# Leaf networks of a depth-4 tree layer: all leaves with a mask, or tokens sorted by leaf

## The reference

```python
x = x + L0_attn(layernorm(x))      # 16 heads, causal
x = x + L0_ffn(layernorm(x))       # trees, then attention 128 wide
x = x + L1_attn(layernorm(x))      # 16 heads
x = x + L1_ffn(layernorm(x))

# L0_ffn: three trees q, k, v on x of 4096 tokens x 128
def _fff(x, node_w, node_b, w1, b1, w2, b2):      # depth 4: 15 nodes, 16 leaves
    cur = 0
    for _ in range(4):
        score = x . node_w[cur] + node_b[cur]
        cur = 2 * cur + 1 + (score >= 0)
    sel = one_hot(cur - 15, 16)
    hidden = relu(x @ w1[l] + b1[l]) * sel[:, l]  # w1[l] 128 x 64, all 16 leaves l
    return sum_l hidden[l] @ w2[l] + sel @ b2     # w2[l] 64 x 128
out = softmax(q k^T / sqrt(128)) v                # per batch of 1024 tokens
```

## Time and profile before

| | |
|---|---|
| median of 3 runs | 1783.16 us (1781.45 to 1785.85) |
| the profiled execution | 1783.86 us, span 1782.1 us |
| busy of the span | PE 91%, DVE 85%, ACT 72%, POOL 46% |
| mean granted TensorE clock | 0.943 |
| bytes moved | 141.89 MB |

### The profile page before, as it was taken

The page is one execution under the profiler, slowest core; times in us unless marked ns, Lnnn a source line. Parts: engine busy times, 40 slices in busy tenths (PEclk is TensorE's granted clock), DMA queues, the critical chain, the costliest instruction groups (busy, mean ns, idle before and its releaser), DMA issues. The chain is left out here.

```text
span 1782.1 us, 47495 instructions
## 1 busy us (share of the span) xinstructions
PE 1613.3 (91%) x18834; PEld 1038.2 (58%) x18858; DVE 1518.7 (85%) x2248; ACT 1276.2 (72%) x2523; POOL 817.8 (46%) x1533
## 2 busy tenths in 40 slices
PE   5599999999976999999899549999999999999966
PEld 3376667666665887877688314444444444444544
DVE  8699999999856999988677768999999999999735
ACT  6488878888834444454565628888989898998955
POOL 5488888888845001000340323444444444444446
PEclk9699999999965999999999868999999999999978
DMA  7522222323172766565000351111121121112031
GB/s 247 207 85 86 87 90 87 98 86 98 52 148 45 97 95 91 93 90 69 0 1 1 144 184 47 56 56 55 59 65 59 52 73 51 60 53 71 26 76 48
DMA packets 119910, 141.89 MB, mean 80 GB/s; under 512 B 22221, under 2 KB 80778, under 8 KB 119690
## 3 DMA queue, kind: packets, MB, share of 16 engines
q1 hardware_dynamic: 119258, 138.79, 30.8%
q10 hardware_dynamic: 432, 0.07, 0.0%
HBM read 92.70 MB, written 44.98 MB: 77 GB/s over the span
## 5 line engine op out<-in xcount | busy, mean ns | idle before, releaser
L888 DVE TENSOR_REDUCE heads_mx<-heads_psM 128x1 f32<-128x1024 f32 x512 | 602.1, 1219 | 48.4 <-PE heads_psM L979 32.2
L959 ACT ACTIVATE heads_probs<-heads_psS 128x512 f32<-128x512 f32 x1024 | 546.1, 601 | 77.7 <-PE heads_psS L1002 71.7
L928 POOL TENSOR_TENSOR heads_masked<-heads_probs,g_tri 128x128 f32<-128x128 f32 x512 | 233.7, 456 | 360.8 <-ACT heads_probs L959 360.7
L654 POOL TENSOR_TENSOR heads_probs<-heads_probs,one_ebias 128x256 f32<-128x256 f32 (+1 forms) x512 | 341.6, 689 | 76.8 <-ACT heads_probs L686 76.1
L615 DVE TENSOR_REDUCE heads_mx<-heads_psM 128x1 f32<-128x1024 f32 (+7 forms) x512 | 348.8, 748 | 23.7 <-PE heads_psM L697 23.0
L686 ACT ACTIVATE heads_probs<-heads_psS 128x512 f32<-128x512 f32 x576 | 316.3, 603 | 67.6 <-PE heads_psS L697 62.4
L979 PE MATMUL heads_psM<-three_kS,three_qS 48*128 48x512 bf16 x1024 | 230.4, 395 | 20.5 <-PEq L2050 11.6
L1002 PE MATMUL heads_psS<-three_qS,three_kS 50*128 50x512 bf16 x1024 | 238.0, 389 | 0.7 <-ACT heads_probs L959 0.3
L1510 ACT ACTIVATE trees_hid_hi<-trees_hid 128x512 fp32r<-128x512 f32 x192 | 121.6, 633 | 152.4 <-DVE trees_hid L1531 151.5
L1531 DVE SCALAR_TENSOR_TENSOR trees_hid<-trees_psH,g_b,trees_chosen 128x512 f32<-128x512 f32 x192 | 143.8, 749 | 31.8 <-DMA trees_chosen<-leaf_choice 15.1
L1027 PE MATMUL heads_psO<-heads_probs,heads_ones_only 128*32 128x128 f32 x1920 | 162.0, 284 | 0.0
(11 more groups left out here) (273 smaller groups left out, 3174.3 us busy)
## 6 DMA issues: line engine op xcount, KB each, us to landing
trees_chosen<-leaf_choice SPq DMA_DIRECT2D x96, 256.0 KB, 7.6
head_outputs<-g_small SPq DMA_DIRECT2D x128, 128.0 KB
one_qS<-q_parts SPq DMA_DIRECT2D x128, 96.0 KB
one_kS<-k_parts SPq DMA_DIRECT2D x128, 96.0 KB
three_qS<-q_parts SPq DMA_DIRECT2D x128, 96.0 KB
three_kS<-k_parts SPq DMA_DIRECT2D x128, 96.0 KB
q_parts<-g_w SPq DMA_DIRECT2D x8, 768.0 KB, 4.6
k_parts<-g_w SPq DMA_DIRECT2D x8, 768.0 KB, 5.8
```

The source lines that it names most:

```text
L654: pool.tensor_tensor(pr[:, a:a + w], pr[:, a:a + w], bass.AP(eb.tensor, eb.offset + NEAR - 1, [list(eb.ap[0]), [-1, w]]), ALU.mult).then_i ...
L888: dve.tensor_reduce(mx[:, n % 2, k:k + 1], psM[k % 2][:, :], AXX, ALU.max, negate=True).then_inc(max_taken, 1)
L928: pool.tensor_tensor(masked[n % 2][:, kb, :], probs[n % 2][:, kb, kb * P:(kb + 1) * P], g["tri"][:, 0:P], ALU.mult).then_inc(near_done, 1)
L959: act.activation(probs[n % 2][:, kb, h * CH:(h + 1) * CH], ring.bank(i)[:, :], ACT.Exp).then_inc(slot_taken, 1)
```

## The change

The leaf networks no longer run over all leaves. `add_projected` keeps the normalized tokens `xn` of all chunks and `sel` of all tiles (`one_of`) for the next stage, no longer makes `x_hi`, `x_lo` and the split weights and biases, and no longer stores `leaf_choice`. SP fills three arrays `sorted_inputs` of 6144 x 128 with zeros instead, in nine transfers of 1 MB, and loads the weights behind them; it waits for both before the stage ends.

`sorted_trees` takes the place of `trees`. Products with triangular tables count how many tokens chose each leaf and rank each token within its leaf. The region of a leaf is padded to whole tiles of 128, and `pos` is each token's row in its tree's sorted array. POOL scatters `xn` to those rows by 96 indexed transfers (3 trees x 32 tiles of 128 rows of 512 bytes). SP loads groups of four sorted tiles; the arrays have 6144 rows whatever the counts are, so there are 12 groups per tree, 36 in all. In a group PE turns the four tiles, multiplies each with the one leaf's `w1` (and with `b1n` for the bias), turns the hidden values and multiplies them with that leaf's `w2s`, which has the second bias as row 65; all in full fp32. The column of the leaf's weights comes from a register that PE loads from `leaf_at` (`which`), once for each product with a leaf's weights. DVE copies the outputs, SP stores them to `sorted_outputs`, and POOL fetches them back in token order by 96 indexed transfers. q and k are turned by PE afterwards and go to `qkT`; v goes to `v_tok` directly.

```diff
 def add_projected(nc, m, g, hand, gather, ins):
...
             gather.load_inverse(sp, B - 1)
-            load_weights(1)
-            load_weights(2)
+            sp.wait_ge(cleared, 2)
+            for f, i in itertools.product(range(FF), range(ZERO_PARTS)):
+                sp.dma_start(bass.AP(g["xs_dram"][f].tensor, i * ZEROS, [[ZERO_PARTS * ZEROS, P], [1, ZEROS]]), zeros[:, :]).then_inc(zeroed, 16)
+            for f in range(FF):
+                load_weights(f)
...
-            for c in range(NCH):
-                store_sel(c)
+            sp.wait_ge(zeroed, 16 * ZERO_PARTS * FF)
+            sp.wait_ge(w_loaded, 16 * (4 * FF + 2))
...
                 act.activation(xnT[:, c % 2, :], psT[c % 2][:, :], ACT.Copy).then_inc(xnT_ready, 1)
-                act.activation(g["x_hi"][:, c * CH:(c + 1) * CH], psT[c % 2][:, :], ACT.Copy).then_inc(high_ready, 1)
...
-def trees(nc, m, g):
+def sorted_trees(nc, m, g):
...
+        @block.sync
+            def load(k):
+                if k % GROUPS == 0:
+                    sp.wait_ge(scattered[k // GROUPS], 16 * NT)
+                if k >= NX:
+                    sp.wait_ge(s["x_turned"], k - NX + 1)
+                sp.dma_start(xg[:, k % NX, :, :], rows(g["xs_dram"], k)).then_inc(x_loaded[k % NX], 16)
+            def store(k):
+                sp.wait_ge(s["y_ready"], k + 1)
+                sp.dma_start(rows(g["ys_dram"], k), yg[:, k % NX, :, :]).then_inc(y_stored[k % NX], 16)
+            for k in range(4):
+                load(k)
+            for k in range(ALL):
+                if k + 4 < ALL:
+                    load(k + 4)
+                store(k)
...
+        @block.gpsimd
...
+            pool.wait_ge(s["pos_ready"], 1)
+            for f in range(FF):
+                for t in range(NT):
+                    pool.indirect_dma_start(g["xs_dram"][f][:, :], bass.IndirectOffsetOnAxis(ap=pos[:, f, t:t + 1], axis=0),
+                                            xn[:, t // TPC, t % TPC, :], None).then_inc(scattered[f], 16)
+            for f in range(FF):
+                for u in range(NX):
+                    pool.wait_ge(y_stored[u], 16 * len([k for k in range((f + 1) * GROUPS) if k % NX == u]))
+                for c in range(NCH):
+                    i = f * NCH + c
+                    if f < 2 and i >= NG4:
+                        pool.wait_ge(s["q_turned"], i - NG4 + 1)
+                    for t in range(c * TPC, (c + 1) * TPC):
+                        out, done = (back[:, i % NG4, t % TPC, :], fetched[i % NG4]) if f < 2 else (g["v_tok"][:, t, :], v_fetched)
+                        pool.indirect_dma_start(out, None, g["ys_dram"][f][:, :], bass.IndirectOffsetOnAxis(ap=pos[:, f, t:t + 1], axis=0)).then_inc(done, 16)
...
+        @block.tensor
...
+            def which(j):
+                return pe.value_load(leaf_at[0:1, j:j + 1], min_val=0, max_val=(LEAVES - 1) * LW)
...
+            def first_layer(k):
...
+                for t in range(TPC):
+                    j = k * TPC + t
+                    out = psH[k % 2][:, t * LW:(t + 1) * LW]
+                    pe.matmul(out, of(j), g["b1n"][:, :], start=True, stop=False)
+                    last = pe.matmul(out, xT[:, k % 2, t * P:(t + 1) * P], g["w1"][:, f, bass.ds(which(j), LW)], start=False, stop=True)
...
+            for k in range(ALL + 3):
+                if k < ALL:
+                    turn(k)
+                if 1 <= k <= ALL:
+                    first_layer(k - 1)
+                if 2 <= k <= ALL + 1:
+                    turn_hidden(k - 2)
+                if k >= 3:
+                    second_layer(k - 3)
+            for i in range(2 * NCH):
+                turn_back(i)
```

More of the change, by code:

```diff
@@ new lines, in keep, with fill @@
+            def keep(t, op, fill, base, pattern, down):
+                pool.wait_ge(s["made"], made[0])
+                pool.affine_select(out=t, in_=t, compare_op=op, fill=fill, base=base, pattern=pattern, channel_multiplier=down).then_inc(s["made"], 1)
+                made[0] += 1
+            def fill(t, value):
+                pool.memset(t, value).then_inc(s["made"], 1)
+                made[0] += 1
+            fill(upper[:, :], 1.0)
+            fill(block_upper[:, :], 1.0)
+            fill(member[:, :], 1.0)
@@ L1434, in _ @@
+            pool.wait_ge(v_fetched, 16 * NT)
         @block.tensor
         def _(pe):
[L1436 to L1449 removed]
@@ new lines, in turn_hidden, with second_layer @@
+            def turn_hidden(k):
+                pe.wait_ge(s["hid_ready"], k + 1)
+                if k >= 2:
+                    pe.wait_ge(s["hidT_ready"], k - 1)
+                for t in range(TPC):
+                    last = pe.transpose(psG[k % 2][0:LW, t * P:(t + 1) * P], hid[:, k % 2, t, :], g["identf"][:, :])
+                last.then_inc(s["hid_turned"], 1)
+            def second_layer(k):
+                f = k // GROUPS
+                pe.wait_ge(s["hidT_ready"], k + 1)
+                if k >= 2:
+                    pe.wait_ge(s["y_ready"], k - 1)
+                for t in range(TPC):
+                    j = k * TPC + t
+                    last = pe.matmul(psO[k % 2][:, t * P:(t + 1) * P], hidT[:, k % 2, t * P:(t + 1) * P], g["w2s"][:, f, bass.ds(which(j) * 2, D)],
+                                     start=True, stop=True)
+                last.then_inc(s["out_done"], 1)
@@ new lines, in turn_back @@
+            def turn_back(i):
+                pe.wait_ge(fetched[i % NG4], 16 * TPC * (i // NG4 + 1))
+                if i >= 2:
+                    pe.wait_ge(s["q_taken"], i - 1)
+                for t in range(TPC):
+                    last = pe.transpose(psQ[i % 2][:, t * P:(t + 1) * P], back[:, i % NG4, t, :], g["identf"][:, :])
+                last.then_inc(s["q_turned"], 1)
+            pe.wait_ge(s["made"], MADE)
+            pe.wait_ge(s["made_v"], 2)
+            for t in range(NT):
+                last = pe.matmul(bank[4][0:W, 0:NT + 1], one_of[:, t, :], after[:, NT - t:2 * NT + 1 - t], start=t == 0, stop=t == NT - 1)
@@ new lines, in _ @@
+            last.then_inc(s["counted"], 1)
+            for i in range(4):
+                pe.matmul(bank[i][:, :], upper[:, :], one_of[:, i * 8:(i + 1) * 8, :].rearrange("p t w -> p (t w)"), start=True, stop=True).then_inc(s["ranked"], 1)
+            pe.wait_ge(s["padded_ready"], 1)
+            pe.matmul(bank[5][0:W, 0:1], block_upper[:, :], padded[:, :], start=True, stop=True).then_inc(s["based"], 1)
+            pe.wait_ge(s["reach_ready"], 2)
+            for t in range(NT):
+                for i in range(2):
+                    last = pe.matmul(bank[6][:, t * TREES:(t + 1) * TREES], selT[0:W, t * P:(t + 1) * P], reach[:, i, t, :], start=i == 0, stop=i == 1)
@@ L1549, in attend_wide @@
+            for k in range(ALL + 1):
+                if k < ALL:
+                    take_hidden(k)
+                if k >= 1:
+                    keep(k - 1)
 def attend_wide(nc, m, g):
```

378 lines of the change are left out of this document (176 added, 202 removed).

## The result

| | before | after |
|---|---|---|
| median of 4 runs each, us | 1783.22 (1781.45 to 1785.85) | 2029.29 (2024.58 to 2030.66) |
| ratio, 95% interval | | 1.1374 (1.1351 to 1.1397) |
| profiled execution: span, us | 1782.1 | 2027.3 |
| mean granted clock of the core | 0.943 | 0.823 |
| trees, from their first instruction to the first of the wide attention, us | 291.6 | 539.8 |

The account below looks back on a forecast made before the run. PE was taken to bound the old trees, DVE close behind. The new stage, 35.4 + 112t + 36G = 457.8 us, is 166.2 longer than 291.6; 1783.9 + 166.2 + 7 = 1957 us, range 1850 to 2110.

Parts of the forecast that it names:

- G: Time of one group of four tiles, 36 in all: 8.0 us, from eight register reads at 0.75 plus 2.0 for turns.
- Opening: Start of the new trees stage, counting and ranking until positions exist and scattering can begin: 20 us, given 15 to 26.
- t: POOL's time for one indexed transfer: 1.2 us, with 112 exposed (32 scatters, 80 fetches), 134 us.
- one by one: Rival: POOL takes each indexed transfer to its landing, t = 3.1 us, kernel 2170 us; chance 0.09.
- as quick as SP: Rival: POOL's 112 exposed transfers at t = 0.34 us, with G = 5.4, kernel 1767 us; chance 0.07.
- First load: After the first tree's scatters: the scatter's landing, 2 us, and a 256 KB load, 3.9 us; 6 us together.
- Its clock decides nothing here: In the groups, PE's real work of 5.1 us at 1.2 GHz was said to fit into the 8 us group.
- The cheap reads: Rival: register reads cost 0.2 to 0.5 us, so loads pace the groups at G = 6.4, kernel 1899 us; chance 0.25.
- filling: Three more iterations of the group loop fill and drain the pipeline with part of the work: 4 us.
- The end: Behind the last fetch, before the next stage: the last landing (3.1 us for 64 KB) and the barrier, 4.4 us.
- Routing: Stage before the trees: nine stores of zeros ahead of the weights on SP's queue lengthen it by 0 to +13, taken +7 us.

Follow-up runs that it names:

- e1: The change with the leaf's number a constant, so PE reads no register in the groups and every tile uses leaf 0; 1955.31 us.
- e8: e5 with PE's group work cut: leaf's first weights stationary, hidden layer comes out turned, bias products and hidden turns dropped; 1812.49 us.
- e4: The change with six unread 128x512 bf16 products added to each group on PE, and one bank for the turned hidden layer; 1933.90 us.
- e6: The change with fifty small unread bf16 products added on PE ahead of the groups; 1961.54 us.
- e13: The change with 12 small unread products on PE ahead of the groups, on the third chip; 2032.25 us.
- e14: The change with 50 small unread products on PE behind the last group, on the third chip; 2034.12 us.
- e11: e12 with the scatters issued in one row, without waits for the groups, and q's turns three groups later; 1836.76 us.
- e12: The kernel of e10 unchanged, timed again on the third chip; 1801.21 us, ratio 1.0103 to the kernel before.
- e5: The change with POOL's scatters of trees k and v paced, four for each group PE has turned; 1967.37 us.
- e10: e8 with q and k turned between the groups and v's 32 fetches moved into the next stage, on the second chip; 1738.02 us.

## Why the prediction was right, and where not

The direction, the chain of links and the range held; the number was 3.6% low, 72 us. That the rest of the sum came out to 3 us is in part luck: G was near by a wrong reason, and errors of both signs cancel. By its own steps:

- **Opening**, 20 us said, 13.5 measured. The 64 products before the positions took 1.9 us and not 6.
- **t**, 1.2 said, 1.26 for a scatter and 1.25 for a fetch. The row of POOL's own pass over a tile came out close, SP's 0.34 and the 3.1 of a landing did not; that a transfer (0.96 busy and 0.30 of "issue") costs what a pass costs is a coincidence as far as any run shows. 32 of them 40.4 us (38.4 said), 80 of them 99.6 (96). Both were exposed exactly as said, POOL idle between its 16th and 17th fetch included. They overlap freely, one every 1.25 us with 2.2 to land, so the rival "one by one" fell, and "as quick as SP" fell by the same row. The Trainium skill (DMA: Bandwidth & Descriptors, Anatomy of one DMA) has a fixed cost of about 2.0 us per transfer. The 2.2 us from issue to landing agree with it, but it is no price for each of a row of transfers when the next is issued before the last has landed.
- **First load**, 6 said, 4.4.
- **G**, 8.0 said, 8.35 measured: a near hit for a wrong reason, and this is the step that failed. The eight reads were put at 0.75 us on PE's path, so that PE would idle in front of them; they took 0.30 beside it, PE did not idle for them, and e1 without them keeps 8.35. What fills the group is PE's own work, which the prediction put at 5.1 us. It read the earlier trace rows, 60-column products "8 in 1.80", as eight products; they are four, of two records each. Even so the row gives 0.45 us a product, 3.6 for the eight and 6.9 for the group. Measured, a product of 64 columns with 128 weights costs 0.62 us at 1.2 GHz, 4.79 for the eight and not 1.8, and the second layer's four took 1.70 and not 1.1. e8 replaces the eight by four of 128 columns with 64 weights and leaves out the hidden layer's turns: 4.2 us a group.
- **"Its clock decides nothing here"** is wrong with it. PE is the bound, so the lower level counts in full: e4 raised the grant to 0.81 and was faster with more work.
- **The cheap reads** rival had its premise right (0.30 us) and its consequence wrong: not the loads but PE's own work took over, at 8.35. Nor do the loads pace at 6.4: e4 has groups 6.0 us apart on the same order of loads and stores. The Trainium skill (DMA: Bandwidth & Descriptors, Latency and other measured facts) has a floor of about 600 ns for a register load; the row here has a median of 299, and the measurement decides.
- **The crawl**, nothing said, +67 us. No rival named a price that a row of POOL's transfers puts on the other engines. Without it the change would have taken 1962 us, and e6 took 1961.5 on a chip where it is absent: the other errors (+13 for G, +6 for t, +6 at the end, -7 opening, -2 first load, -2 filling, -11 routing) come to +3 on the 1957.
- **The end**, 4.4 said, 10.5 from the last fetch to the next stage. It was 10.5 to 10.7 us in every run that ends with fetches; the last landing is about 2.5 us of it (the median of such a fetch in e6 and e8), and what fills the rest stays open.
- **Routing**, +7 said, -4 measured. As said, the stage ends when SP's transfers have landed: its last load is issued at 552.36 us and awaited until about 555.9, while ACT's last copy ends at 555.1. But the row of transfers was shorter: the zeros were expected at 259 GB/s, and 516 to 520 us ran at 426. And the other runs end the same stage 1.4 us earlier to 8.0 later, so the -4 is one draw from a spread that reaches beyond 0. A row of SP's timeline, and one of its waits:

```profile
552.36 0.43 SPq L1185 DMA_DIRECT2D g_mu<-in_L_ffn_mu_k  x1
...
SPq L1187 <- DMA g_mu<-in_L_ffn_mu_k: 3.1, 1, 3.1
```

## What to carry over

Count what the trace counts: a full-precision product is two records, and its price depends on the clock's level and on how many weights go in for how few columns; read it from a row of the same shape before calling an engine hidden. A row of indexed transfers on one in-order engine costs its issue time each (1.25 us here for 128 rows of 512 bytes), not its latency, so put it beside the work that it does not depend on: moving 48 of them from behind the last product took 57 us off. And time a kernel that leans on such transfers on more than one chip, and more than once, before a few per cent are believed.

## What the runs showed of the hardware that was not expected

- **Other engines can crawl while POOL issues indexed transfers, and not everywhere.** One kernel took 1738 us on one chip and 1801 on another; the kernel before, with no such transfer, 1780 and 1782. The change ran with the crawl, as did all four kernels of the third set, and none of the first two sets' (e1, e4 and e6 among them, which issue 64 scatters beside the groups without a pause). In it PE, ACT and DVE slow down together, nearly always with "issue" as the only reason shown, while POOL keeps its 1.26 us. In the change it begins some 18 us after PE's first turn, and again 18 us after the first of the 16 fetches. What starves them stays open. Instructions arriving too late would look like this, but the counts do not settle it: between 590 and 675 us the two instruction queues moved one packet in the change, e13 and e14, two in e11 and five in e12, which all crawl, and three in e1 and e5, four in e4 and e6, seven in e10, which do not. Few packets can also only follow from engines that use few instructions.
- PE busy 100% of a stretch of 240 us (660 to 900) with narrow full-precision products was granted 0.50 all through (e1).
- The stores of zeros in 8 KB runs went at 426 GB/s, well over the 259 of the 2 MB load, which is its bytes by the whole time to landing. The stretch in the change:

```profile
516.00:520.00 4.00, 4.00 (x20) 4.00 (x20) 2.16 (x9) 3.19 (x8) 2.51 (x2) 0.50 1.01 426
```
